# Graph kernel on one Trainium2 core: x also given with features on partitions, its norm summed on TensorE, the counts stored from ScalarE's queue

## The chip, the cores and the metric

One core of one Trainium2 chip runs the whole program. The metric is the device time of one execution in microseconds (us); the kernel before takes 937.81 us as the median of 3 runs (936.04 to 939.39). The engines are called as the profile calls them: PE (TensorE, with PEld for its weight loads), DVE (VectorE), ACT (ScalarE), POOL (GpSimd) and SP (SyncE, which here only issues DMAs). "SPq" and "ACTq" are the parts of SP and ACT that issue.

## What is computed

Two graph layers over 6250 nodes with 128 features and 200000 edges that are sorted by `dst`, each followed by a layer norm:

```python
h = x @ W + b_W;  xi, xj = split(h, 2)
xji = xj[src] + (edge_attr @ W_e + b_We)
xji = xji / (in_degree[dst] + 1e-6)
x1  = layernorm(x + xi + segment_sum(xji, dst))          # layer 0

h   = x1 @ W1                                            # layer 1, with self loops
out = segment_sum(h[src] * dinv[src] * dinv[dst], dst) + b1
y   = leaky_relu(batchnorm(out) * gamma + beta)
return layernorm(x1 + y)
```

What the change touches belongs to layer 0: the own part `x + xi`, which is one product of `x` with (W + identity), and the split of `x` into two float16 parts (high and low), which needs a power of two as a common scale.

## The kernel before

The 6250 nodes lie in 25 blocks (NB) of 256 receivers; `x` is kept in SBUF as 49 tiles (HS) of 128 nodes. For each block the kernel builds a matrix of counts, how many edges go from each sender to each receiver of the block: for 16 steps ("slots", `s` = 0 to 15) DVE makes pairs of one-hot tiles (`one_hots`, L616 and L619, one pair of instructions for two slots, in a ring of 6 slots), PE multiplies them (`count`, L858, 8 matmuls for a slot), and ACT writes the result as bf16 into `counts` (`pair_out`, L1065). There are two buffers `counts`, for even and odd blocks. While block b is counted, PE multiplies the counts of block b-1 with the split x (`product`, L876, and L884 for the parts of layer 1 that can be done early), and sums the edges' features (`edges`, L895). The counts of each block also go to HBM (`counts_kept`), since layer 1 reads them again; `pair_out` of block b, slot 0, must wait until the store of block b-2 has landed, as it writes the same buffer. After block 24 comes a stretch in which PE gathers layer 1 from the kept counts (`gather_z`, L951), and then the output.

The order on each engine is the order in which the functions are called in its loop over b and s; nothing is planned by a scheduler. Every engine runs its own list and waits at semaphores. What the change touches:

- **The start, before block 0.** SP loads rows of `dst` (`load_rows`, L301), weights and the first third of x. `find_below` and `pick_rows` (DVE L557, L562), `find_rows` (PE L911), `count_row` and `start_of` (DVE L569 to L576) find where the edges of a block start; POOL then gathers a window of `dst` and `src` (L465), and `make_keys` (DVE L582 to L602), `turn_keys` (PE L921) and `tables` (ACT L1089) make the keys from which `one_hots` works.
- **The own part.** x lies with nodes on partitions, so PE turns each tile (`turn_x`, L972), ACT copies it from PSUM (`x_turned`, L1137), PE multiplies it with the weights (`own_product`, L981), and ACT copies the result into `zown` (`own_out`, L1142); 13 groups of up to 4 tiles (OWN), four of them before block 0 and the rest one per slot of block 0. One PSUM bank, `j_ps`, takes all the products.
- **The scale.** DVE takes the largest absolute value of each row (`largest`, L646, three pieces of x), PE turns the column of largest values (L1007), DVE makes four numbers of it (`scales`, L655 to L663), PE spreads them over the partitions (L1010) and DVE copies them (`spread_scales`, L668). Then ACT writes the high part of each third of x (`split_high`, L1130) and DVE the low part (`split_low`, L681).
- **SP's list for block b:** rows for block b+4, then `start_values`, `load_destinations` (L333), `keep_inverse` (L370), `keep_counts(b-1)` (L349), the first half of the edges' features (`load_edges`, L342), and the second half. The second half of block 0 waits for the last `split_low`, because its buffer is the one that holds x.

## Time and profile before

| | us |
|---|---|
| median of 3 runs | 937.81 |
| the profiled execution, its own time | 936.68 |
| the span that the profile covers | 934.6 |
| PE busy in it | 883.9 (95%) |
| DVE busy | 676.6 (72%) |
| ACT busy | 450.3 (48%) |
| POOL busy | 349.4 (37%) |

The profile is one execution, taken by the hardware profiler. It gives the busy time of each engine, the clock that TensorE was granted, the groups of instructions by line with the idle time before them and what ended it, and for any stretch the instructions in order of time. Times count from the start of the span. 2.1 us of the execution's time lie outside the span. A matmul's end is modelled, so neighbouring matmuls overlap in the list; the distance of their starts is what they cost.

### The profile page before, as it was taken

What the parts mean: (1) busy time and instruction counts of PE and PEld (TensorE: products, weight loads), DVE (VectorE), ACT (ScalarE), POOL (GpSimd) and SP (SyncE); (2) the same over time, 40 slices, a digit from 0 to 9 for tenths busy, and PEclk for the clock granted to TensorE, in tenths of its full rate; (3) what the DMA queues carried; (4) which work ended last, traced back from release to release, by engine and by line L of the source; (5) the groups of instructions that cost most, each with busy time, mean ns of one, the idle gap of its engine ahead of it and who ended that gap; (6) DMA issues with size and microseconds to landing.
All of it is one profiled execution on the core that took longest, in us unless ns stands there. A gap on an engine that the chain in (4) does not pass through costs nothing.

```text
span 934.6 us, 30500 instructions
## 1 busy us (share of the span) xinstructions
PE 883.9 (95%) x12210; PEld 791.2 (85%) x12210; DVE 676.6 (72%) x1249; ACT 450.3 (48%) x983; POOL 349.4 (37%) x401
## 2 busy tenths in 40 slices
PE   4867999999999999999999999999999999999995
PEld 4756888888988898989899999999988888888874
DVE  6999899999999998899888899888842111112255
ACT  3764666656666665556565556565542000000026
POOL 2236444455554444455334455434332011112200
PEclk8988999999999999999999999999999999999998
DMA  6428999998879788777878758678667897779654
GB/s 180 110 83 296 361 345 320 317 342 290 313 247 319 284 311 283 229 229 241 253 264 277 223 185 301 214 274 282 209 216 299 343 358 279 272 260 326 249 155 136
DMA packets 96762, 244.77 MB, mean 262 GB/s; under 512 B 39560, under 2 KB 64838, under 8 KB 90726
## 3 DMA queue, kind: packets, MB, share of 16 engines
q1 hardware_dynamic: 95014, 239.46, 73.7%
q0 software_dynamic: 1600, 3.28, 1.4%
q8 instruction: 100, 1.64, 0.8%
q14 instruction: 48, 0.39, 0.2%
HBM read 183.85 MB, written 58.85 MB: 260 GB/s over the span
## 4 chain that ended last, share of the span: by engine, by line
PE 85%; DVE 5%; issue 3%; ACT 3%; DMA 1%; SPq 1%; ACTq 0%; DVEq 0%
PE x_ps L876 26%; PE pair_ps L951 19%; PE pair_ps L858 13%; PE e_ps L895 10%; PE x_ps L884 9%; PE j_ps L933 2%; PE j_ps L981 2%; DVE lo_oh L616 1%; DVE key_oh L619 1%; PE pair_ps L960 1%; PE j_ps L934 1%; ACT counts L1065 1%; PE u_vps L1409 1%; DMA counts_kept<-counts 1%; DMA streams<-in_x 1%
## 5 line engine op out<-in xcount | busy, mean ns | idle before, releaser
L1065 ACT CAST counts<-pair_ps 128x784 bf16<-128x784 f32 x391 | 315.3, 817 | 251.5 <-PE pair_ps L858 244.1
L876 PE MATMUL x_ps<-counts,xsplit 128*128 128x256 bf16 (+1 forms) x2450 | 307.5, 271 | 0.0
L616 DVE TENSOR_TENSOR lo_oh<-counter,lo_t 128x2048 bf16<-128x2048 bf16 x196 | 252.3, 1287 | 53.9 <-PE pair_ps L858 52.5
L876 PEld LDWEIGHTS x_ps<-counts,xsplit 128*128 128x128 f16 x2450 | 222.1, 98 | 29.3 <-issue 7.1
L858 PE MATMUL pair_ps<-key_oh,lo_oh 128*128 128x100 bf16 x3128 | 207.8, 209 | 22.5 <-ACT counts L1065 15.4
L858 PEld LDWEIGHTS pair_ps<-key_oh,lo_oh 128*128 128x128 bf16 x3128 | 182.8, 98 | 36.9 <-issue 15.0
L619 DVE TENSOR_TENSOR key_oh<-counter,key_t 128x1600 bf16<-128x1600 bf16 x196 | 196.4, 1002 | 0.0
L895 PE MATMUL e_ps<-streams 128*32 128x128 f32 x3528 | 106.9, 274 | 0.1
L884 PE MATMUL x_ps<-counts,zown 128*128 128x256 bf16 (+1 forms) x840 | 105.9, 269 | 0.1
L951 PE MATMUL pair_ps<-streams,zown 128*128 128x256 bf16 x878 | 99.0, 273 | 0.0
L895 PEld LDWEIGHTS e_ps<-streams 128*32 128x32 f32 x3528 | 93.3, 110 | 4.8 <-issue 1.0
L476 POOL TENSOR_SCALAR quot<-deg 128x2 f32<-128x2 f32 x25 | 5.7, 226 | 243.2 <-DVE junk L595 231.5
L951 PEld LDWEIGHTS pair_ps<-streams,zown 128*128 128x128 f16 x878 | 85.8, 98 | 11.4 <-issue 0.2
L884 PEld LDWEIGHTS x_ps<-counts,zown 128*128 128x128 f16 x840 | 76.1, 97 | 10.3 <-issue 2.9
L492 POOL TENSOR_SCALAR bias<-linear,share 128x128 f32<-128x128 f32 x50 | 76.0, 1532 | 14.7 <-DVE vo L705 13.7
L951 PE MATMUL pair_ps<-counts,zown 128*128 128x256 bf16 (+1 forms) x732 | 79.9, 268 | 0.0
L951 PEld LDWEIGHTS pair_ps<-counts,zown 128*128 128x128 f16 x732 | 69.3, 98 | 9.2
L1313 ACT ACTIVATE u_co<-u_co 128x1 f32<-128x1 f32 x1 | 0.2, 203 | 156.0 <-DVEq L1351 156.0
L825 DVE TENSOR_TENSOR s_mem<-pair_ps,key_oh 128x256 f32<-128x256 f32 (+1 forms) x23 | 9.6, 418 | 83.8 <-PE pair_ps L951 81.3
L639 DVE TENSOR_TENSOR streams<-iota,ekeys 128x1152 f32<-128x1152 f32 x49 | 67.5, 1377 | 2.7 <-PE e_ps L895 0.3
L833 DVE TENSOR_TENSOR xsplit<-pair_ps,key_oh 128x256 f32<-128x256 f32 (+1 forms) x25 | 10.5, 419 | 58.7 <-PE pair_ps L960 57.0
L507 POOL TENSOR_TENSOR streams<-streams,key_oh 128x512 bf16<-128x512 bf16 x13 | 15.0, 1151 | 84.9 <-DMA streams<-counts_kept 84.9
(181 smaller groups left out, 890.6 us busy)
## 6 DMA issues: line engine op xcount, KB each, us to landing
streams<-in_edge_attr SPq DMA_DIRECT2D x196, 576.0 KB, 9.1
counts_kept<-counts SPq DMA_DIRECT2D x10, 1600.0 KB, 9.1
streams<-counts_kept SPq DMA_DIRECT2D x6, 1600.0 KB, 6.5
counts<-counts_kept SPq DMA_DIRECT2D x4, 1600.0 KB, 7.1
counts_kept<-counts SPq DMA_DIRECT2D x2, 3136.0 KB, 12.7
streams<-counts_kept SPq DMA_DIRECT2D x2, 3136.0 KB, 14.8
edst<-in_dst SPq DMA_DIRECT2D x196, 4.5 KB
streams<-in_x SPq DMA_DIRECT2D x3, 1024.0 KB, 5.7
```

Of the source, the lines that this page charges most:

```text
L492: last = g.tensor_scalar(bias[:, t, :], bje, share[:, 2 * b + t:2 * b + t + 1], None, ALU.mult)
L616: dv.tensor_tensor(lo_oh[:, ring, :, :, :].rearrange("p r w k t -> p (r w) k t"), counter[:, :, :].unsqueeze(1).to_broadcast([P, g, P, 2]) ...
L619: dv.tensor_tensor(key_oh[:, ring, :, :, :].rearrange("p r w k t -> p (r w) k t"), counter[:, 0:KW, :].unsqueeze(1).to_broadcast([P, g, KW ...
L639: dv.tensor_tensor(e_oh[g][:, :, :], iota[:, 0:EC].unsqueeze(1).to_broadcast([P, EG * EJ, EC]), ekeys[:, k].unsqueeze(2).to_broadcast([P, ...
L858: last = nc.tensor.matmul(pair_ps[at % 2][:, half_of, col:col + KW], lo_oh[:, at % RING, w // 2, :, w % 2], key_oh[:, at % RING, w // 2, : ...
L876: last = nc.tensor.matmul(x_ps[:, 0, 0:n], xsplit[:, q // 2, q % 2, :], by_hi[:, q // 2, :], start=(q == 0), stop=(q == 2 * HS - 1))
L884: last = nc.tensor.matmul(x_ps[:, 1, 0:n], zsplit[:, z // 2, z % 2, :], by_hi[:, z // 2, :], start=(z == 0), stop=(z == early(k) - 1))
L895: last = nc.tensor.matmul(e_ps[EC * c:EC * (c + 1), g, :], e_oh[g][:, c * EJ + j, :], ebuf[g][:, c, j, :], start=(j == 0), stop=(j == EJ - 1))
L933: nc.tensor.matmul(out, sx[:, t:m:2], wj, start=True, stop=False)
L951: last = nc.tensor.matmul(z_ps[i % 2][:, 0:n], zsplit[:, q // 2, q % 2, :], by_hi[:, q // 2, :], start=(q == early(b)), stop=(q == 2 * HS ...
L981: last = nc.tensor.matmul(j_ps[:, k, :], xT[m % 2][:, k, :], wi, start=True, stop=True)
L1065: a.copy(out.rearrange("p h (g n) -> p h g n", g=2), pair_ps[at % 2][:, :, 0:4 * KW].rearrange("p g (n h) -> p h g n", h=HI)[:, 0:HS]).the ...
```

## The change

1. The host hands x over in two more layouts, both as 49 tiles: `x_rows` (nodes on partitions, as before) and `x_columns` (features on partitions). SP loads both, the columns first, straight into `zown`; the memset of x's last tile on POOL goes.
2. The own part takes its tiles from `x_columns`: `turn_x` and `x_turned` go, and the products alternate between two PSUM banks (`j_ps` and `e_ps`), each followed by `own_out` into the place that the columns held. One group stands ahead of block 0, the other twelve in slots 0 to 11.
3. The scale comes from the norm of x: PE multiplies the upper bf16 half of each column tile with itself and adds up all 49 products in one bank (`sum_squares`), DVE sums the diagonal (`add_squares`), PE adds it over the partitions (one matmul with ones), and DVE makes the scales on all partitions (`scales`). `largest` in block 0 goes; `row_largest` reads the high parts in blocks 16, 18 and 20 instead.
4. The splits stand earlier: ACT's in slots 9, 12, 15 (were 11, 13, 15), DVE's in 14, 17, 20 (were 16, 18, 20).
5. `find_below` and `pick_rows` of blocks 2 and 3, with ACT's and PE's parts, move ahead of the first own product.
6. `keep_counts(b-1)` moves from SP's queue to ACT's, at slot 0 of block b, ahead of `pair_out`.
7. Rows are loaded one turn sooner, at another place of SP's list; `count_row` and `start_of` move from slots 9 and 10 to 11 and 12.

```diff
-LARGEST_AT = (None, 2, 4)
-TOP_AT, SCALES_AT, SPREAD_AT = 5, 8, 12
-HIGH_AT, LOW_AT = (11, 13, 15), (16, 18, 20)
+NORM_AT, TOTAL_AT, SCALES_AT = 7, 6, 10
+HIGH_AT, LOW_AT = (9, 12, 15), (14, 17, 20)
+ROWS_CHECKED_AT = (16, 18, 20)
-OWN_FIRST = 4
+SQUARED_FIRST, OWN_FIRST = 4, 1
+SQUARED_IN = {1: (4, 5, 6, 7), 3: (8, 9, 10, 11, 12)}
...
+def load_pieces(sp, out, table, loaded, pieces):
     for k in pieces:
+        at = piece_tiles(k)
+        sp.dma_start(out[:, at.start * F:at.stop * F], table[:, at.start * F:at.stop * F]).then_inc(loaded[k], 16)
...
+        own_ps = [j_ps, e_ps]
+        squares_ps, norm_ps = x_ps[:, 0, 0:P], x_ps[:, 1, 0:1]
+        upper_halves = zown[:, :].bitcast(BF16).rearrange("p (h n q) -> p h n q", n=P, q=2)[:, :, :, 1]
...
             for b in range(2):
                 load_rows(sp, b)
-            sp.dma_start(wi, W0[:, 0:F]).then_inc(S["wi_in"], 16)
-            load_inputs(sp, {"x": xf}, x, S, range(1))
+            load_pieces(sp, columns, x_columns, S["columns_in"], range(1))
             for b in range(2, ROW_RING):
                 load_rows(sp, b)
+            sp.dma_start(wi, W0[:, 0:F]).then_inc(S["wi_in"], 16)
             load_weights(sp, {"wj": wj, "we": we, "bi": bi, "bj": bje, "be": be_t[:, :]}, W0, b0, We, be, S)
             sp.wait_ge(win_in[0], 32)
-            load_inputs(sp, {"x": xf}, x, S, range(1, len(X_PIECES)))
+            load_pieces(sp, columns, x_columns, S["columns_in"], range(1, len(X_PIECES)))
+            load_pieces(sp, xf, x_rows, S["x_in"], range(len(X_PIECES)))
...
-                if 1 <= b <= NB - 2:
-                    keep_counts(b - 1)
...
+            def add_squares():
+                dve.wait_ge(S["squares_summed"], 1)
+                step(dv.tensor_tensor(x1_mem[:, 0, :], squares_ps, ident[:, :], ALU.mult))
+                dv.tensor_reduce(out=norm[:, :], in_=x1_mem[:, 0, :], axis=AX.X, op=ALU.add).then_inc(S["norm_ready"], 1)
...
+            def row_largest(k):
                 at = piece_tiles(k)
+                step(dv.tensor_reduce(out=rowmax[:, at], in_=xsplit[:, at, 0, :], axis=AX.X,
+                                      op=ALU.max, apply_absolute_value=True))
...
+            def sum_squares(m):
+                columns_here(m)
+                h, n = OWN[m]
+                for k in range(h, h + n):
+                    last = nc.tensor.matmul(squares_ps, upper_halves[:, k, :], upper_halves[:, k, :], start=(k == 0), stop=(k == HS - 1))
+                last.then_inc(S["columns_squared"], 1)
...
             def own_product(m):
                 h, n = OWN[m]
+                columns_here(m)
                 pe.wait_ge(S["weights_ready"], 1)
-                pe.wait_ge(S["xT_out"], m + 1)
-                reach(pe, S["own_added"], m)
+                reach(pe, S["own_added"], m - 1)
                 for k in range(n):
-                    last = nc.tensor.matmul(j_ps[:, k, :], xT[m % 2][:, k, :], wi,
-                                            start=True, stop=True)
+                    last = nc.tensor.matmul(own_ps[m % 2][:, k, :], own[:, h + k, :], wi, start=True, stop=True)
...
-            for b in range(2):
+            for b in range(ROW_RING):
                 find_rows(b)
-            for m in range(OWN_FIRST):
-                turn_x(m)
-                if m >= 1:
-                    own_product(m - 1)
+            for m in range(SQUARED_FIRST):
+                sum_squares(m)
+                if m < OWN_FIRST:
+                    own_product(m)
             turn_keys(0)
-            for b in range(2, 4):
-                find_rows(b)
-            own_product(OWN_FIRST - 1)
...
+            def keep_counts(k):
+                act.wait_ge(S["pair_out"], first_slot(k) + slots(k))
+                at, n = early(k) // 2 * cols(k), HS * cols(k)
+                act.dma_start(scratch["counts"][k * P:(k + 1) * P, at:n], counts[k % 2][:, at:n])\
+                   .then_inc(counts_kept[k % 2], 16)
...
+                    if s == 0 and 1 <= b <= NB - 2:
+                        keep_counts(b - 1)
                     if b < NB and s < slots(b):
                         pair_out(b, s)
```

How the instructions of one engine stand in its list, before and with the change, at three places. First PE, from its start to the second slots of block 0. The old list (L911 finds rows, L972 turns x, L981 is the own product, L921 and L922 turn the keys, L858 counts a slot):

```order
L911 MATMUL pair_ps<-rows,pick 128x129 x2
L972 MATMUL x_ps<-ident,streams 128x128 x4
L972 MATMUL e_ps<-ident,streams 128x128 x4
L981 MATMUL j_ps<-linear,x_mem 128x128 x4
L972 MATMUL x_ps<-ident,streams 128x128 x4
L981 MATMUL j_ps<-linear,s_mem 128x128 x4
L972 MATMUL e_ps<-ident,streams 128x128 x4
L981 MATMUL j_ps<-linear,x_mem 128x128 x4
L921 MATMUL keys_ps<-ident,key 128x128
L922 MATMUL keys_ps<-ident,lo 128x128
L911 MATMUL pair_ps<-rows,pick 128x129 x2
L981 MATMUL j_ps<-linear,s_mem 128x128 x4
```

The new list (L886 finds rows, L948 squares, L960 is the own product, L896 and L897 turn the keys, L831 counts):

```order
L886 MATMUL pair_ps<-rows,pick 128x129 x4
L948 MATMUL x_ps<-zown 128x128 x4
L960 MATMUL j_ps<-linear,zown 128x128 x4
L948 MATMUL x_ps<-zown 128x128 x12
L896 MATMUL keys_ps<-ident,key 128x128
L897 MATMUL keys_ps<-ident,lo 128x128
L831 MATMUL pair_ps<-key_oh,lo_oh 128x100 x8
L960 MATMUL e_ps<-linear,zown 128x128 x4
L831 MATMUL pair_ps<-key_oh,lo_oh 128x100 x8
L948 MATMUL x_ps<-zown 128x128 x16
L960 MATMUL j_ps<-linear,zown 128x128 x4
L831 MATMUL pair_ps<-key_oh,lo_oh 128x100 x8
```

Ahead of the keys stand four tiles of the own part instead of twelve, no tile is turned, and all four row products come first; 16 and 17 of the squares stand in slots 1 and 3 of block 0.

Second DVE, block 0 from its second pair of one-hots to the first low part. The old list (L616 and L619 a pair of one-hots, L646 the rows' largest values, L655 to L663 the scales, L668 their copy, L681 the low part; the ten instructions of the keys and the repeated pairs are left out):

```order
L646 TENSOR_REDUCE rowmax<-streams 128x17
L650 TENSOR_REDUCE pmax<-rowmax 128x1
L616 TENSOR_TENSOR lo_oh<-counter,lo_t 128x2048
L619 TENSOR_TENSOR key_oh<-counter,key_t 128x1600
L616 TENSOR_TENSOR lo_oh<-counter,lo_t 128x2048
L619 TENSOR_TENSOR key_oh<-counter,key_t 128x1600
L655 TENSOR_REDUCE top<-keys_ps 1x1
L656 TENSOR_SCALAR expo<-top 1x1
```

The new list from its fifth pair (L597 and L600 a pair, L625 and L626 the diagonal, L630 to L638 the scales):

```order
L625 TENSOR_TENSOR x_mem<-x_ps,ident 128x128
L626 TENSOR_REDUCE norm<-x_mem 128x1
L597 TENSOR_TENSOR lo_oh<-counter,lo_t 128x2048
L600 TENSOR_TENSOR key_oh<-counter,key_t 128x1600
L597 TENSOR_TENSOR lo_oh<-counter,lo_t 128x2048
L600 TENSOR_TENSOR key_oh<-counter,key_t 128x1600
L630 COPY top<-x_ps 128x1
L631 TENSOR_SCALAR sound<-top 128x1
```

The reductions over 2048 and 2176 elements are gone from between the pairs of block 0; two instructions over 128 elements stand in their place.

Third ACT, from the ninth slot of block 0 to the first slots of block 1. The old list (L1065 writes counts, L1130 the high part, L1151 and L1152 rows for a later block, L1083 a root):

```order
L1151 ACTIVATE heads<-rows_i,shift 128x2
L1152 ACTIVATE rows<-rows_i,shift 128x128
L1065 CAST counts<-pair_ps 128x49x16
L1130 ACTIVATE xsplit<-streams,xscale 128x16x128
L1065 CAST counts<-pair_ps 128x49x16 x2
L1130 ACTIVATE xsplit<-streams,xscale 128x16x128
L1065 CAST counts<-pair_ps 128x49x16 x2
L1130 ACTIVATE xsplit<-streams,xscale 128x17x128
L1065 CAST counts<-pair_ps 128x49x16 x3
L1083 ACTIVATE quot<-quot 128x2
```

The new list (L1033 writes counts, L1105 the high part, L1112 copies an own product, L1121 and L1122 rows, L1046 the store):

```order
L1105 ACTIVATE xsplit<-streams,xscale 128x16x128
L1033 CAST counts<-pair_ps 128x49x16
L1112 COPY zown<-e_ps 128x512
L1121 ACTIVATE heads<-rows_i,shift 128x2
L1122 ACTIVATE rows<-rows_i,shift 128x128
L1033 CAST counts<-pair_ps 128x49x16
L1112 COPY zown<-j_ps 128x128
L1033 CAST counts<-pair_ps 128x49x16
L1105 ACTIVATE xsplit<-streams,xscale 128x16x128
L1033 CAST counts<-pair_ps 128x49x16 x3
L1105 ACTIVATE xsplit<-streams,xscale 128x17x128
L1046 DMA counts_kept<-counts 128x12544
```

All three high parts now stand in block 0, the first of them ahead of six slots' counts, and the store of block 0's counts follows the last of them on ACT itself.

## Rows read from the trace of the kernel before

**Rows 1.** Busy time by stretch: PE, PEld, DVE, ACT, POOL (instructions), PE clock, DMA share, GB/s.
```profile
24.00:25.00 1.00, 0.94 (x7) 0.81 (x4) 1.00 (x1) 0.92 (x2) 0.00 (x0) 0.50 0.09 5
88.00:89.00 1.00, 0.25 (x4) 0.28 (x5) 1.00 (x2) 1.00 (x2) 0.92 (x2) 0.50 1.04 428
150.00:175.00 25.00, 24.23 (x398) 21.75 (x397) 24.75 (x45) 16.78 (x35) 12.97 (x15) 1.00 0.90 322
400.00:425.00 25.00, 25.00 (x397) 22.83 (x396) 21.59 (x33) 14.37 (x30) 11.31 (x12) 1.00 0.74 233
```

**Rows 2.** DVE in order of time: start, us, line, what, [idle before <-releaser].
```profile
11.14 0.23 DVE L582 TENSOR_SCALAR bit_i<-gsrc 128x128 int32<-128x128 int32 x1 [0.75 <-DMA gsrc<-in_src,start_i]
16.87 0.29 DVE L557 TENSOR_SCALAR below<-even,heads 128x128 f32<-128x128 f32 x1 [3.88 <-ACT rows L1152]
...
19.54 1.22 DVE L616 TENSOR_TENSOR lo_oh<-counter,lo_t 128x2048 bf16<-128x2048 bf16 x1
...
23.61 2.28 DVE L646 TENSOR_REDUCE rowmax<-streams 128x16 f32<-128x2048 f32 x1
...
29.66 2.41 DVE L646 TENSOR_REDUCE rowmax<-streams 128x17 f32<-128x2176 f32 x1
...
43.63 0.16 DVE L668 COPY xscale<-keys_ps 128x4 f32<-128x4 f32 x1 [1.78 <-PE keys_ps L1010]
...
48.49 2.35 DVE L681 SCALAR_TENSOR_TENSOR xsplit<-streams,xscale,xsplit 128x2048 f16<-128x2048 f32 x1 [0.50 <-ACT xsplit L1130]
...
63.46 1.36 DVE L616 TENSOR_TENSOR lo_oh<-counter,lo_t 128x2048 bf16<-128x2048 bf16 x1
...
87.32 1.12 DVE L619 TENSOR_TENSOR key_oh<-counter,key_t 128x1600 bf16<-128x1600 bf16 x1
...
95.35 0.35 DVE L569 TENSOR_SCALAR_CACHE_REDUCE row_junk<-keys_ps,th 128x128 bf16<-128x128 f32 x1 [1.44 <-ACT lo_t L1090]
...
99.67 1.27 DVE L616 TENSOR_TENSOR lo_oh<-counter,lo_t 128x2048 bf16<-128x2048 bf16 x1 [0.40 <-PE pair_ps L858]
```

**Rows 3.** PE in order of time, in block 0 and at the start of block 2.
```profile
18.48 1.95 PE L981 MATMUL j_ps<-linear,s_mem 128*128 128x128 f32 x8
...
29.48 1.13 PE L981 MATMUL j_ps<-linear,x_mem 128*128 128x128 f32 x8 [0.41 <-ACT x_mem L1137]
30.44 0.60 PE L972 MATMUL e_ps<-ident,streams 128*128 128x128 f32 x4
...
88.75 0.83 PE L858 MATMUL pair_ps<-key_oh,lo_oh 128*128 128x100 bf16 x8 [4.55 <-ACT counts L1065]
```

**Rows 4.** ACT in order of time: the first high part, and the start of block 2.
```profile
46.45 2.01 ACT L1130 ACTIVATE xsplit<-streams,xscale 128x2048 f16<-128x2048 f32 x1
...
87.80 1.53 ACT L1065 CAST counts<-pair_ps 128x784 bf16<-128x784 f32 x2 [5.61 <-issue]
```

**Rows 5.** SP's queue in order of time: block 0's edges, and the first store of counts.
```profile
30.68 34.96 SPq L342 DMA_DIRECT2D streams<-in_edge_attr  x8
...
75.47 0.43 SPq L349 DMA_DIRECT2D counts_kept<-counts  x1
```

**Rows 6.** DMA issues from 75 to 100 us, KB each, median us to landing.
```profile
counts_kept<-counts SPq DMA_DIRECT2D x2, 3136.0 KB, 12.7
```

**Rows 7.** SP's issues of the store, then of rows: ns min/median/max.
```profile
L349 SPq DMA_DIRECT2D counts_kept<-counts x23: 430/431/1789, 75.5 to 659.3; - x23
L301 SPq DMA_DIRECT2D rows_i<-in_dst x23: 398/442/2570, 0.7 to 509.4; - x23
```

**Rows 8.** Waits of all engines, 100 to 150 us, then 500 to 600: total, times, longest.
```profile
DVE lo_oh L616 <- PE pair_ps L858: 2.7, 3, 2.1
DVE lo_oh L616 <- PE pair_ps L858: 13.2, 8, 2.7
```

**Rows 9.** ACT, then PE, at a later block's start.
```profile
455.41 1.56 ACT L1065 CAST counts<-pair_ps 128x784 bf16<-128x784 f32 x2
457.47 0.53 PE L858 MATMUL pair_ps<-key_oh,lo_oh 128*128 128x100 bf16 x8
```

197 lines of the change are left out of this document (77 added, 120 removed).

## The prediction

> **What bounds the kernel now.** I read the busy time by stretch first [rows 1]; the reader should see that the bound changes: from 150 to 175 us DVE is busy 24.75 of 25 us, from 400 to 425 us only 21.59, while PE is then busy for all 25.00. So up to about 200 us DVE sets the pace, behind it PE, and a microsecond won on DVE early moves everything after it, since PE starts each block when its one-hots are there. I then followed DVE in order of time [rows 2]. It starts block 0 at 19.54 us and from there to 93.8 us stands still only twice for more than a tenth: 1.78 us for PE's answer to the scales and 0.50 us for ACT's first high part. The point I measure against is 63.46 us, where the last low part is done and the pair of slot 6 in block 1 starts; from there DVE's list is the same before and after, but for small moves.
>
> Later PE shows its one long stop, 4.55 us ahead of 88.75 [rows 3]. ACT, for which it waits, itself stood 5.61 us and began at 87.80 [rows 4]. The view calls that "issue", but ACT's list has a wait there for the store of block 0's counts. SP issued that store only at 75.47, since its list was held in block 0's edges from 30.68 for 34.96 us [rows 5]; with 12.7 us to landing [rows 6] it lands at about 88.2, or a little before. So the store is what PE waited for.
>
> **Start of block 0.** Before: keys at 11.14, done 1.85 us later at 12.99; then DVE stood 3.88 us until 16.87, because ACT's copies of the turned x stood ahead of the rows of blocks 2 and 3; 2.67 us of row work; first pair at 19.54 [rows 2]. Now that row work starts as soon as the rows land. The piece of columns has the size of the piece of x and should land at the same 8 us; rows and weights are queued behind it, so I put the row work at 9.0 to 10.4, the weights' four instructions (1.1 us) to 11.6, the keys to 13.4, the two counts of rows (1.3 us) beside PE's and ACT's work on the keys, and the first pair at 14.9. **-4.6 us.** Bounds: -5.2 if the keys start at 11.14 as before, -3.5 if one own product at the low clock (1.95 us for four tiles [rows 3]) lies ahead of the keys in full.
>
> **Work taken from DVE in block 0.** The second and third `largest` (2.28 and 2.41 us [rows 2], with the reduction behind the third 5.0 in all): **-5.0**. The first, at 8.1, lay beside the wait for the gather and is worth nothing. The wait for the scales goes with its copy (2.07, of which 1.78 is the wait) and so do eight small instructions (1.08); in come two instructions over 128 elements and six small ones, 1.55 together by their like: **-1.6**. The 0.50 us for the first high part goes with its neighbours, **-0.6**. Sum so far -11.8.
>
> **What is late next.** PE and ACT. PE's slot in block 0 before was an own product and a turn, 0.96 us from start to start (29.48 to 30.44), and a slot's count of 0.37, drawn out to 2.34 by waits on ACT [rows 3]. Without the turns and with two banks it is 0.96 + 0.37 = 1.33 us for 12 slots. The 33 squares of slots 1 and 3 have no row of their own. The lower bound is a 128-column matmul of 16 bits, 0.05 us, the upper one a turned tile of 32 bits, 0.11 (0.44 for four, behind [rows 3]'s 0.60). I take 0.055, since they are 16-bit: 1.8 us. The clock also counts: it was 0.50, the lower of its levels (1.2 GHz), at 24 to 25 us [rows 1], after PE had idled around 17 us, and at that level an own product took 1.95 against 1.13 [rows 3]. I let PE run 4 us from 17 us at that level. PE's slot 9 is then counted at 33.3, two slots behind DVE. ACT writes it, copies a product (about 0.5, as PE's wait of 0.41 for such a copy tells) and only then makes the first high part (2.01 [rows 4]), done at 37.3. DVE is ready for it at 35.4: 1.9 us of new wait. Before the second high part it waits some 0.7 more, and for a free place of the ring and the diagonal 0.9. **+3.5**; bounds 0 and 6. At my point the sum is -8.3: 55.2 instead of 63.46.
>
> **The store.** Now on ACT behind block 0's last count, at about 47 us, where DMA is nearly idle, and landed long before block 2. The 4.55 us of PE go, and the clock, which had fallen to 0.50 at 88 us [rows 1], stays up. But that isn't the gain. PE would next want the one-hots of slot 4, and DVE, busy throughout, has them only at 88.4 (87.32 and 1.12 [rows 2]). What is gained is what DVE stood still in consequence: 1.44 and 0.40 [rows 2] and the longest wait on PE in 100 to 150 us, 2.1 [rows 8]: **-3.9**. Bounds: 0 and -6.9 (the stop and 2.3 us of slow clock in full).
>
> **Costed at nothing.** Each store now takes ACT one issue, 0.43 us as on SP [rows 7], and a wait for its own last count. Behind it stand the next counts, for which PE waits two slots later: at a later block's start ACT has the first of two done at 456.2 (half of 1.56 after 455.41), and PE takes it up at 457.47 [rows 9], so 1.2 us cover it; without cover 23 x 0.43 = 10 us. The three `row_largest` (2.3 us each) fall in blocks 16, 18 and 20, where DVE waits for PE 13.2 us in 100 [rows 8]; without that cover, 6.9. The 3.1 MB of second layout run from 11 to 28 us, ahead of any edge's feature that is wanted. Rows a turn sooner, and the row counts two slots later, are waited for by nobody.
>
> **Sum.** -8.3 - 3.9 = -12.2 against the profiled 936.7 (span 934.6 and 2.1 outside), so 924.5; the median of the runs lies 1.1 above the profiled run, so 925.6.
>
> **A rule against it.** The store's gain rests on it being issued some 28 us sooner, by SP's rows [rows 5]. The Trainium skill ("DMA: Bandwidth & Descriptors", "Issuing engines are not separate DMA queues") says that DMAs from several engines run on the same 16 DMA engines and that issuing from more than one only saves issue time. By that alone the move would be worth nothing, and the sum be -8.3. The trace doesn't contradict the rule, it shows a case outside of it: what held the store was a wait in SP's list.
>
> **Rivals.**
> - *Clean overlap:* PE and ACT keep up, the 3.5 us of new waits don't come. For it: ACT loses its turned copies. Against it: 16 counts at 0.77, 12 copies at 0.5 and the three high parts (2.0 to 2.1, [rows 4]) give ACT 24.5 us of work, to DVE's 22. 922.1.
> - *The store brings nothing:* DMA was at 1.04 of its share at 88 us [rows 1], and if the edges of blocks 1 and 2 hold PE there in the store's place, only -8.3 is left: 929.5.
> - *The gather of block 1 comes late:* 5.2 MB of x now run while it does. DVE wants it at 18.9; if it landed only with the last of x, near 26, 7.5 us of the gain would go: 933.1. Against it: POOL issues it ahead of those pieces, for which SP waits until 11.1.
> - *PE's clock stays low through block 0:* twice 19.3 us from 17 gives 55.5 for its last count instead of about 51, and with the store's gain nothing is left: 938. Against it: PE has fewer gaps than before, and before the clock was back by 27 us.
> - *Slower:* the issue on ACT holds it longer than the cover. One of 23 on SP took 1.79 us, and one of its issues of rows 2.57 [rows 7]. It decides from 1.2 + 12.2 / 23 = 1.7 us for each store. At 2.6 it costs 1.4 x 23 = 32, so 957. Against it: the median is 0.431 [rows 7], and ACT has a queue to itself.
>
> **Chances.** Forecast 0.50; clean overlap 0.17; store brings nothing 0.15; late gather 0.08; slow clock 0.05; slower 0.05. The range goes from 919 (3 us under clean overlap, for the bounds of the start and the store) to 933, and leaves out the last two and half of the late gather. No change is within 0.3% (2.8 us), about what a measurement of this kernel can tell: slow clock, 0.05; faster 0.90; slower 0.05.
>
> **What would show it.** In the new profile: first pair of one-hots near 14.9 us; all low parts done near 55; DVE's waits in block 0 on ACT's high parts, some 3 us, and none on a matmul for the scales; no stop of PE near the start of block 2, and a clock of 1.00 there; the store issued from ACT near 47 us with 0.43 us an issue; PE without idle time from 400 us on, as before. It is wrong if DVE waits on the gather in block 0, if ACT's issues exceed 1 us, or if PE shows waits on ACT at each block's start behind 400 us.

## The result, and the profile after

The changed kernel takes **943.59 us** as the median of 20 runs (936.97 to 950.21); the kernel before, run beside it on the same chip, 937.51 (20 runs, 935.10 to 941.11). The ratio is 1.0064, 95% interval 1.0047 to 1.0081: **slower by 0.64%**, where 925.6 and 90% for faster were forecast. The profiled execution took 947.89 us, with a span of 946.1, of which PE is busy 884.7 (883.9 before), DVE 675.2 and ACT 444.7. So none of these three has more to do; PE waits more. (POOL shows 392.3 against 349.4, but PE waits for it nowhere, and DVE 1.4 us at the start, as before.) Two steps of the forecast can be looked up at once.

**The start came out as forecast.** DVE in order of time, the columns being those of [rows 2]:

```profile
15.06 1.23 DVE L597 TENSOR_TENSOR lo_oh<-counter,lo_t 128x2048 bf16<-128x2048 bf16 x1 [0.67 <-ACT lo_t L1064]
...
25.43 0.29 DVE L625 TENSOR_TENSOR x_mem<-x_ps,ident 128x128 f32<-128x128 f32 x1 [0.32 <-PEq L952]
...
28.57 1.23 DVE L597 TENSOR_TENSOR lo_oh<-counter,lo_t 128x2048 bf16<-128x2048 bf16 x1 [0.49 <-PE pair_ps L831]
...
37.56 2.35 DVE L655 SCALAR_TENSOR_TENSOR xsplit<-streams,xscale,xsplit 128x2048 f16<-128x2048 f32 x1 [1.35 <-ACT xsplit L1105]
...
42.72 2.35 DVE L655 SCALAR_TENSOR_TENSOR xsplit<-streams,xscale,xsplit 128x2048 f16<-128x2048 f32 x1 [0.77 <-ACT xsplit L1105]
...
53.03 2.47 DVE L655 SCALAR_TENSOR_TENSOR xsplit<-streams,xscale,xsplit 128x2176 f16<-128x2176 f32 x1
55.43 1.35 DVE L597 TENSOR_TENSOR lo_oh<-counter,lo_t 128x2048 bf16<-128x2048 bf16 x1
```

The first pair stands at 15.06 (forecast 14.9, before 19.54), the pair behind the last low part at 55.43 (forecast 55.2, before 63.46). The new waits shown, 0.32 + 0.49 + 1.35 + 0.77 = 2.9 us, are those that the forecast put at 3.5; a fifth, 0.54 us on ACT for a root at 31.86, it had not named.

**The stop of block 2 is gone.** Its slot 0 is counted at 73.58 with a wait of 0.63 us, where PE stood 4.55 [rows 3]; its slot 5 at 81.52, 13.1 us ahead of before. Then comes what the forecast did not have. PE in order of time:

```profile
73.58 0.52 PE L831 MATMUL pair_ps<-key_oh,lo_oh 128*128 128x100 bf16 x8 [0.63 <-ACT counts L1033]
...
81.52 0.53 PE L831 MATMUL pair_ps<-key_oh,lo_oh 128*128 128x100 bf16 x8
88.40 4.07 PE L870 MATMUL e_ps<-streams 128*32 128x128 f32 x72 [6.35 <-issue]
92.40 1.34 PE L849 MATMUL x_ps<-counts,xsplit 128*128 128x256 bf16 x7
```

PE stands 6.35 us, and no engine or DMA is named as what ended it: "issue" means a wait for nothing that the profile shows. The 72 matmuls behind the stop take 4.00 us from start to start instead of the 2.1 of elsewhere; the granted clock from 88 to 92 us is 0.50, the lower of the two levels (1.2 GHz), after the engine had stood. There are ten stops with "issue" as their end, 17.7 us in all, between 82 and 560 us. The waits of the whole execution (engine, tile and line, releaser: total, times, longest), first of the changed kernel, then of the one before:

```profile
PE e_ps L870 <- issue: 14.7, 8, 6.4
PE x_ps L849 <- issue: 1.9, 1, 1.9
PE pair_ps L831 <- issue: 1.0, 1, 1.0
```

```profile
PE pair_ps L858 <- issue: 1.2, 1, 1.2
```

They are of two kinds.

**Two stand at the head of a group of edge matmuls** ("x72"), 6.35 us at 88.40 and 2.13 at 177.65, 8.5 in all. There the program has a wait: `edges` waits until the edges' features have landed. The profile doesn't name it; in this execution it gives no landing time for these loads. The row of the DMA issues, which before ended in a median of 9.1 us:

```profile
streams<-in_edge_attr SPq DMA_DIRECT2D x196, 576.0 KB
```

SP issued the first group's edges of block 1 from 69.10 on, ACT the store of block 1's counts (3.1 MB) at 73.47, with the edges still on their way. SP's and ACT's queue in order of time:

```profile
69.10 2.16 SPq L331 DMA_DIRECT2D streams<-in_edge_attr  x4
```

```profile
73.47 0.33 ACTq L1046 DMA_DIRECT2D counts_kept<-counts  x1
```

The kept trace also has each increment of the semaphore for which `edges` waits, 64 for the four loads of a group. The last one for this group came at 88.31 us, 0.09 us before PE went on at 88.40; for the second stop it came at 177.56, again 0.09 us ahead of 177.65. So both are waits for edges. p_slot4 below shows such a stop with its name.

**The eight others, 9.2 us, lie inside groups**, with 1, 2, 4, 4, 20, 31, 53 and 70 matmuls of the group to go, where the program has no wait. The busy time by stretch of the changed kernel, cut at stops (columns of [rows 1]):

```profile
118.00:142.30 24.30, 23.43 (x372) 20.94 (x372) 23.12 (x44) 16.40 (x34) 15.76 (x14) 1.00 0.93 314
...
186.00:211.60 25.60, 22.95 (x373) 20.52 (x373) 22.45 (x43) 15.41 (x31) 15.80 (x14) 1.00 0.92 307
211.60:238.10 26.50, 24.25 (x373) 21.58 (x372) 24.17 (x44) 15.15 (x30) 15.79 (x14) 0.94 0.88 299
238.10:281.00 42.90, 40.85 (x619) 36.90 (x620) 37.73 (x73) 27.19 (x55) 22.98 (x24) 1.00 0.86 281
281.00:307.20 26.20, 25.11 (x372) 22.54 (x372) 22.55 (x44) 16.43 (x34) 11.31 (x14) 1.00 0.86 263
```

Between two of them lie 744 to 746 matmuls and weight loads, or 1239, five thirds of that. (The stop at 88.40 is off this grid, 909 from the next one, and so is that at 177.65, with 1013 before it and 233 behind; both are of the first kind.) With the waits at semaphores, which stand in PE's list as instructions of their own, the steps are 768 and 1280, or 3 and 5 times 256. Data and buffers don't come in steps of 256 instructions; the instructions themselves do, if they are fetched in pieces of fixed size. The DMA queues of the changed kernel (packets, MB, share of 16 engines' span):

```profile
q1 hardware_dynamic: 89338, 193.20, 64.3%
q10 hardware_dynamic: 3312, 49.48, 12.3%
q0 software_dynamic: 1600, 3.28, 1.3%
q8 instruction: 100, 1.64, 0.7%
q14 instruction: 49, 0.39, 0.2%
```

q8 carries "instruction": 100 packets of 16384 bytes, 1.64 MB in all, which is 64 bytes for each of 256 instructions. The trace has the time of each packet. The stop that ends at 118.12 us ends 1.5 us after one of them (115.77 to 116.65), and so do the seven others, 1.2 to 1.5 us after; at 88.40 and 177.65 the last packet of q8 is 6.6 to 6.7 us old. The same holds for the experiments below: of the 100 stops that their table counts as within groups, in all kernels together, 99 end 1.2 to 1.7 us after a packet of q8 and stand a whole number of 256 instructions apart in PE's list (the other is one of 0.24 us in j_half_store). So PE's instructions come by DMA, and these stops are **instruction fetches that come late**. q10, 3312 packets of 15 KB on average, is new: the stores that ACT issues, before a part of q1.

Where the time is lost: block 4's first group of edges stands at 165.81 us (168.14 before), block 6's at 224.63 (219.43), block 10's at 333.95 (323.74), and behind that the two kernels run in step, 10 us apart (block 15's at 472.51 and 462.46). The gain of some 13 us at 82 us, and 10 more, go between there and 330 us, where the DMA engines have least to spare: their share from 150 to 200 us is 0.95, from 400 to 425 it is 0.82.

### The profile page after: what moved, and what is told of

Its sections match the earlier page's. It is cut to its first block, busy times and chain, and to the rows that moved or that the text cites. A ratio compares the mean times of both kernels' runs of the same rounds, so it can differ in the third digit from the quotient of the medians.

```text
span 946.1 us, 30473 instructions
## 1 busy us (share of the span) xinstructions
PE 884.7 (94%) x12209; PEld 791.2 (84%) x12209; DVE 675.2 (71%) x1245; ACT 444.7 (47%) x970; POOL 392.3 (41%) x400
## 3 DMA queue, kind: packets, MB, share of 16 engines
q10 hardware_dynamic: 3312, 49.48, 12.3%
q8 instruction: 100, 1.64, 0.7%
## 4 chain that ended last, share of the span: by engine, by line
PE 85%; DVE 5%; issue 4%; ACT 3%; DMA 2%; SPq 0%; ACTq 0%; DVEq 0%
PE x_ps L849 26%; PE pair_ps L926 17%; PE pair_ps L831 14%; PE e_ps L870 11%; PE x_ps L857 9%; PE j_ps L908 2%; DVE key_oh L600 1%; ACT counts L1033 1%; PE j_ps L909 1%; DMA key_oh<-sums_z 1%; PE pair_ps L935 1%; DVE lo_oh L597 1%; PE u_vps L1376 1%; PE j_ps L960 1%; DMA rows_i<-in_dst 1%
## 5 line engine op out<-in xcount | busy, mean ns | idle before, releaser
L1033 ACT CAST counts<-pair_ps 128x784 bf16<-128x784 f32 x391 | 315.6, 817 | 271.5 <-PE pair_ps L831 250.7
L597 DVE TENSOR_TENSOR lo_oh<-counter,lo_t 128x2048 bf16<-128x2048 bf16 x196 | 247.0, 1260 | 69.6 <-PE pair_ps L831 68.4
L831 PE MATMUL pair_ps<-key_oh,lo_oh 128*128 128x100 bf16 x3128 | 207.3, 208 | 20.5 <-ACT counts L1033 11.1
L831 PEld LDWEIGHTS pair_ps<-key_oh,lo_oh 128*128 128x128 bf16 x3128 | 182.2, 98 | 34.6 <-issue 16.5
L600 DVE TENSOR_TENSOR key_oh<-counter,key_t 128x1600 bf16<-128x1600 bf16 x196 | 198.8, 1014 | 0.0
L870 PE MATMUL e_ps<-streams 128*32 128x128 f32 x3528 | 112.2, 279 | 14.8 <-issue 14.7
L870 PEld LDWEIGHTS e_ps<-streams 128*32 128x32 f32 x3528 | 97.0, 112 | 19.1 <-issue 15.4
L473 POOL TENSOR_SCALAR bias<-linear,share 128x128 f32<-128x128 f32 x50 | 72.5, 1456 | 14.6 <-DVE vo L679 13.7
L619 DVE TENSOR_TENSOR streams<-iota,ekeys 128x1152 f32<-128x1152 f32 x49 | 67.1, 1369 | 3.2 <-PE e_ps L870 0.8
L475 POOL TENSOR_TENSOR bias<-bias,linear 128x256 f32<-128x256 f32 x25 | 55.6, 2225 | 2.1
L806 DVE TENSOR_TENSOR xsplit<-pair_ps,key_oh 128x256 f32<-128x256 f32 (+1 forms) x25 | 10.5, 419 | 58.6 <-PE pair_ps L935 57.1
```

The source lines that it names most:

```text
L473: last = g.tensor_scalar(bias[:, t, :], bje, share[:, 2 * b + t:2 * b + t + 1], None, ALU.mult)
L475: g.tensor_tensor(bias[:, :, :], bias[:, :, :], bi.unsqueeze(1).to_broadcast([P, 2, F]), ALU.add).then_inc(S["bias_ready"], 1)
L597: dv.tensor_tensor(lo_oh[:, ring, :, :, :].rearrange("p r w k t -> p (r w) k t"), counter[:, :, :].unsqueeze(1).to_broadcast([P, g, P, 2]) ...
L600: dv.tensor_tensor(key_oh[:, ring, :, :, :].rearrange("p r w k t -> p (r w) k t"), counter[:, 0:KW, :].unsqueeze(1).to_broadcast([P, g, KW ...
L619: dv.tensor_tensor(e_oh[g][:, :, :], iota[:, 0:EC].unsqueeze(1).to_broadcast([P, EG * EJ, EC]), ekeys[:, k].unsqueeze(2).to_broadcast([P, ...
L831: last = nc.tensor.matmul(pair_ps[at % 2][:, half_of, col:col + KW], lo_oh[:, at % RING, w // 2, :, w % 2], key_oh[:, at % RING, w // 2, : ...
```

## The experiments

The theories after this first look. **Q, the second queue:** stores from ACT's queue run beside the edges' loads of SP's instead of in one line with them, and edges and instruction fetches come late. **T, the moment:** wherever it is issued, the store now goes ahead of the destinations and edges of its block instead of behind them. Each kernel ran five rounds, beside the kernel before, whose median lay between 935.76 and 938.10 from batch to batch; so ratios to it are compared, of which 0.001 is 0.94 us. The last column has PE's waits on "issue" between 40 and 760 us in the one profiled execution, which can lie several us off the median (c's is the longest of 12): those at the head of a group of edges, and all others, which nearly always stand within a group. Waits that the profile names as a DMA are not in it: 1.5 us in e, 1.3 in o, 0.5 in i, 5.3 in p.

| kernel | stores of counts | ratio to before (95%) | median us | stops, head + within |
|---|---|---|---|---|
| before | SP, behind destinations | 1 | 937.51 | 0 + 1.2 |
| changed | ACT, block's end | 1.0064 (1.0047 to 1.0081) | 943.59 | 8.5 + 9.2 |
| a_sp_store | SP, old place | 0.9928 (0.9906 to 0.9949) | 931.15 | 0 + 3.7 |
| b_act_store (before's x) | ACT, block's end | 1.0176 (1.0139 to 1.0214) | 953.92 | 4.9 + 10.5 |
| c_small_packets | ACT, 4 KB packets | 1.0012 (0.9996 to 1.0028) | 939.26 | 5.1 + 10.2 |
| d_late_store | ACT, slot 8 | 1.0070 (1.0045 to 1.0095) | 944.54 | 3.7 + 3.1 |
| e_sp_head | SP, head of its turn | 1.0001 (0.9987 to 1.0015) | 935.10 | 0 + 6.6 |
| **f_first_on_act** | block 0's on ACT, others SP, old place | **0.9888** (0.9872 to 0.9903) | **925.47** | 0 + 2.9 |
| g_before_small (before's x) | ACT, 4 KB packets | 1.0099 (1.0077 to 1.0120) | 943.84 | 0 + 5.5 |
| i_before_head (before's x) | SP, head | 1.0173 (1.0159 to 1.0187) | 952.30 | 0 + 9.3 |
| j_half_store | half of each ACT, half SP | 0.9938 (0.9913 to 0.9963) | 932.72 | 3.2 + 6.3 |
| k_late_blocks | as f, from block 10 on ACT | 0.9906 (0.9876 to 0.9937) | 929.68 | 0 + 5.1 |
| l_sp_tail | as f, SP behind both groups of edges | 1.2965 (1.2924 to 1.3006) | 1216.82 | 0 + 0 |
| m_sp_between | as f, SP between the groups | 1.0097 (1.0065 to 1.0130) | 945.93 | 0.5 + 1.0 |
| n_first_small | as f, 4 KB packets | 0.9875 (0.9857 to 0.9892) | 925.63 | 0 + 2.0 |
| o_head_small | as e, 4 KB packets | 0.9997 (0.9975 to 1.0019) | 936.99 | 0.6 + 7.5 |
| p_slot4 | ACT, slot 4 | 0.9986 (0.9960 to 1.0012) | 934.36 | 0 + 5.1 |

### The two halves of the change

a_sp_store: the changed kernel with the store back in SP's list; b_act_store: the kernel before with only the store moved.

```diff
# a_sp_store, against the changed kernel: on ACT
-                    if s == 0 and 1 <= b <= NB - 2:
-                        keep_counts(b - 1)
# on SP
+                if 1 <= b <= NB - 2:
+                    keep_counts(b - 1)
                 if b < NB:
                     load_edges(b, 0, starts)
# b_act_store, against the kernel before: the same lines the other way round
```

> The changed kernel with one part undone: the stores of the counts are issued by SP again, at their old place. Theory Q (the store on a queue of its own is served between the packets of the edges' features and of PE's instructions, one of its packets of some 22 KB against one of theirs of 4.6 KB or less, and so makes PE wait): the waits of PE called issue fall from 17.6 us to under 3, the start keeps its gain of 8 us, the stall at block 2 is partly back, 926 to 932. Theory X (the new start or SP's new order costs it): it stays at 940 or more. Theory R (the DMA engines are simply short of throughput once the blocks start sooner): 936 to 942, PE's waits for edges stay.

> The kernel before with only the stores of the counts moved to ACT's queue at slot 0. Theory Q: the stall ahead of 88 us goes, but waits of PE called issue come up in blocks 1 to 9, 15 us or more in sum, so slower than before, 941 to 950. Theory X: 932 to 936, since the store alone is harmless. Theory R: between, 934 to 939.

The part on x alone is a gain of 0.72% (6.7 us), the store alone a loss of 1.8% (16.5 us; 953.9 is above the 941 to 950 of theory Q), with stops of both kinds: 4.85 us at the head of a group at 97.28, then within groups 1.61, 2.63 and 2.30. In a_sp_store the first edges stand at 54.53 us against 62.80, the forecast's 8.3 to the tenth; at 400 us 5.6 of them are left. The two halves don't simply add: in the changed kernel the same move of the store costs 12.8 us (1.0064 against 0.9928), not 16.5.

### Packets, and a later slot

c_small_packets and g_before_small leave a gap of 128 bytes behind every eight tiles of kept counts in HBM, so that a store goes out in packets of 4 KB instead of 12.8 (the late blocks) to 25.1 (the first two). d_late_store issues from ACT at slot 8 of the block instead of 0.

```diff
# c, g
-                act.dma_start(scratch["counts"][k * P:(k + 1) * P, at:n], counts[k % 2][:, at:n])
+                for kept, part, q in kept_parts(scratch["counts"][k * P:(k + 1) * P, :], at // BN):
+                    ours = counts[k % 2][:, part]
+                    act.dma_start(kept, ours if q is None else ours.rearrange("p (g q) -> p g q", q=q))
# d
-                    if s == 0 and 1 <= b <= NB - 2:
+                    if s == 8 and 1 <= b <= NB - 2:
```

> The changed kernel, the stores still on ACT's queue at slot 0, but the kept counts laid out in HBM with 128 bytes of padding behind every 8 tiles, so that a packet holds 4 KB and not 25 KB (two issues for each store and each load). Theory Q, if the size of the packets is what matters: most of PE's waits go, 924 to 934. If only the number of queues matters, or theory R: as the changed kernel, 940 to 946.

> The changed kernel with the store on ACT's queue at slot 8 of the next block instead of slot 0, about when SP issued it before. Theory Q: the packets still come between, so the waits only move, 938 to 946. A theory T (it is the time of the store, in front of the edges that are due next, that matters): waits fall, 926 to 934.

> The kernel before with the stores on ACT's queue at slot 0, kept with padding so that a packet holds 4 KB. The large packets gave 953.9. Theory Q with the size of packets as a part of it: 940 to 948, a third to two thirds of the 17 us come back, as 4 to 5 of the changed kernel's 12 did. If the size doesn't matter: 950 to 957.

Small packets give back 4.9 us (c) and 7.2 us (g): in g the stops fall from 15.3 to 5.5 us, in c, whose profile is 3.0 us shorter than the changed kernel's, from 17.7 to 15.3. That is part of the loss at most; c lies between its two expectations. d's time is in theory Q's range, but not for Q's reason: its stops fall to 6.7, and still it is no faster. ACT in order of time:

```profile
135.92 1.53 ACT L1033 CAST counts<-pair_ps 128x784 bf16<-128x784 f32 x2 [3.66 <-DMA counts_kept<-counts]
```

The store of block 2, issued at 120.50, lands at 135.9, 15.4 us later, and ACT has to wait for it before it writes that buffer again; seven such waits make 11.7 us. Slot 8 is too late for a store that takes this long beside the edges.

### The moment, on one queue

All stores from SP's queue, at the head of its turn, so ahead of the destinations and edges, nearly as early as from ACT (block 0's at 56.8 us instead of 45.2, block 1's at 77.4 instead of 73.5): e_sp_head with the changed kernel's x, i_before_head with that of before. And f_first_on_act: only the store of block 0 from ACT, where no edges run, the other 22 in the old place.

```diff
# e, i, on SP
             for b in range(NB + 2):
+                if 1 <= b <= NB - 2:
+                    keep_counts(b - 1)
                 if b < NB:
                     starts = start_values(b)
# f, on ACT; SP keeps those of blocks 1 to 22 ahead of load_edges(b, 0)
+                    if s == 0 and b == 1:
+                        keep_first_counts()
```

> The changed kernel with all stores back on SP's queue, but each at the head of SP's turn, ahead of the values, destinations and edges. Theory Q (interleaving of two queues costs it, the early store itself is good): the stall at block 2 goes and nothing comes between the packets, the start's 8 us and most of the 3.9 are kept, 924 to 928. Theory T (a store ahead of the edges costs it, on whatever queue): 932 or more, PE waits for edges.

> The kernel before with only its stores moved to the head of SP's turn: the stall ahead of 88 us alone. Theory Q, with the price of 3.9 us from the prediction: 932 to 935.5. If the stall was worth nothing, or SP's list then becomes late: 936 or more.

> The changed kernel with only block 0's store on ACT's queue (issued near 45 us, with nothing else in flight) and the 22 others on SP's at their old place. Theory Q: one store that meets no other traffic costs nothing and takes the stall away, 924 to 929. If a second queue costs by being used at all, or if starting block 2 sooner only brings PE to edges that aren't there: 931 or more.

f is 1.12% under the kernel before, the most of all but n_first_small below, which equals it, and it **shows the two gains of the forecast together**: 3.7 us more than a_sp_store (by the intervals, 1.3 to 6.2), for the stop at block 2 that was put at 3.9. At the same place in its program PE doesn't stop. PE in order of time, the group that stood at 88.40 above:

```profile
81.67 0.53 PE L839 MATMUL pair_ps<-key_oh,lo_oh 128*128 128x100 bf16 x8
82.12 2.17 PE L878 MATMUL e_ps<-streams 128*32 128x128 f32 x72
```

Fetches still come late at the same places: f stops at 108.96, 133.02, 195.75 and 220.53 us, with the same 1, 20, 2 and 4 matmuls to go as in the changed kernel at 118.12, 142.44, 211.73 and 238.21, for 0.21, 0.17, 0.84 and 1.72 us instead of 1.53, 0.66, 1.94 and 1.79.

Against f, moving the 22 others costs 16.5 us (0.0176). e says how this divides: 10.6 us (0.0113) come without a second queue, by the moment, 5.9 (0.0063) with the queue. The division is rough, since e's stores also start some us later than the changed kernel's. But **Q alone is refuted** (it had 924 to 928 for e), **and T alone too**, as long as those few us are not what makes the 5.9. The heads of groups tell what the second queue does: on one queue (e) the store of block 1 stands behind the edges that were issued before it, and PE waits for edges once, 1.5 us; from ACT it runs beside them, and the wait is 8.5. i is as slow as b, but its trace has a cause of its own. ACT in order of time:

```profile
84.82 0.30 ACT L1151 ACTIVATE heads<-rows_i,shift 128x2 f32<-128x2 int32 x1 [10.93 <-DMA rows_i<-in_dst]
```

Here the rows, 64.5 KB that SP issues at 66.84, stand in the queue behind the edges (64.17 to 66.25) and 3.1 MB of store, and ACT, which turns them into numbers in the same block, waits 10.93 us for them; there are six such waits between 40 and 760 us, 17.2 us in all, about i's whole loss of 16.2. In e, whose rows are loaded a turn sooner, they are missing. The part of the change that I had costed at nothing is what an early store on this queue needs.

### How much of it, and when

j_half_store: of each later store half the bytes from ACT at the block's end, half from SP in the old place. k_late_blocks: as f, but from block 10 on (about 330 us) all of it from ACT.

```diff
# j, on ACT; SP stores half:n in the old place, and waits count 32 for a block
+                half = (at + n) // 2
+                for a0, a1 in [(at, half), (half, n)][:1 if k else 2]:
+                    act.dma_start(scratch["counts"][k * P:(k + 1) * P, a0:a1], counts[k % 2][:, a0:a1])
# k, on ACT
+                    if s == 0 and (b == 1 or 11 <= b <= NB - 2):
+                        keep_counts(b - 1)
```

> As the kernel with block 0's store alone on ScalarE's queue (925.5), but of every later store half of the bytes leave from ScalarE's queue at the block's end and the other half from SyncE's at the old place behind the destinations. Moving all of the bytes cost 18.1 us (943.6). Theory Q+T (it is the volume that runs ahead of and beside the edges and beside the instruction fetches): between, about half, 931 to 938. If the mere presence of a second queue decides: nearly the whole, 940 to 944. If the harm needs the long store (8 us of all engines) to outlast something: 925 to 928.

> As the kernel with block 0's store alone on ScalarE's queue (925.5), and the stores of blocks 10 to 22 (issued from about 330 us on) there too: 14 of 23 stores moved. The trace of the changed kernel lost its time between 82 and 300 us, where the DMA engines are busy 90 to 100% of the time. Theory load (a moved store only hurts where the engines are full): 925 to 928. Theory price per store (0.8 us for each of 22): 935 to 937.

Half of the bytes costs 4.7 us over f, 28% of the whole, with stops of 9.5: the mere presence of a second queue isn't it, the volume counts. The 13 late stores cost 1.7 us (the intervals of k and f overlap: anything from nothing to 5), the nine early ones the rest of the 16.5. That is 0.1 us for a late one and some 1.6 for an early one, so no fixed price per store. The early ones are larger (2.1 to 3.1 MB, against 1.6 to 2.0), but not by as much; that the fuller DMA engines make the rest fits their shares above, and is not shown by itself.

### Later places on SP's queue

l_sp_tail stores behind both groups of edges, m_sp_between behind the first.

```diff
# m; l has the same two lines behind load_edges(b, 1)
                     load_edges(b, 0, starts)
+                if 2 <= b <= NB - 2:
+                    keep_counts(b - 1)
```

> As the kernel with block 0's store alone on ScalarE's queue (925.5), the others on SyncE's queue at the end of the turn, behind both groups of edges. Theory order (what is behind the store in the queue is delayed by it; next is then the next block's destinations, some 10 us later): 924 to 927. If the store comes too late for the counts' buffer two blocks on, ScalarE waits for its landing at block starts: 930 to 945.

> As before, the others between the two groups of edges on SyncE's queue: the first group no longer waits behind the store. Theory order: 924 to 927, the best place if the first edges are what is late; if the old place was only good because of its time, no change within 0.3% (923 to 928).

I had expected these to be at least as good as f. m has 945.9, outside of both its ranges, and l is slower by 30%, by the cause that its second theory named, but far above its 930 to 945. Waits of l_sp_tail, and ACT in order of time in it:

```profile
PE pair_ps L839 <- ACT counts L1041: 252.2, 41, 15.8
...
ACT counts L1041 <- DMA counts_kept<-counts: 248.2, 21, 15.9
```

```profile
156.70 1.53 ACT L1041 CAST counts<-pair_ps 128x784 bf16<-128x784 f32 x2 [15.72 <-DMA counts_kept<-counts]
```

21 of 22 stores land too late for their buffer, by 11.8 us on average, and it seems to feed itself: the second group of edges waits for a buffer that PE frees only when it goes on. m has eight such waits, 15.3 us, and hardly any stop of the other kind (1.5 us). The old place, behind the destinations and ahead of the edges, is thus between two losses: earlier, fetches and loads are held up; later, the counts' buffer.

### Packets once more

With the length of the packets still open, at the good place and at the early one on one queue (edit as in c, with the placing of f and e):

> As the kernel with block 0's store alone on ScalarE's queue (0.9888 of before), but the counts are kept in HBM with a gap of 128 bytes behind every eight tiles, so that the packets of the stores are 4 KB instead of about 15 to 22 KB. On SyncE's queue, in the old place. If the length of a packet is what another queue's fetch waits behind, whatever the place: 0.984 to 0.988, a little better, as fetch stops of 2.9 us are left to win. If it matters only where stores run beside the edges: 0.987 to 0.991. If more packets cost in themselves: above 0.992.

> As the kernel with all stores at the head of SyncE's turn (1.0001 of before), with packets of 4 KB. One queue, the same early moment as in the changed kernel. If long packets at that moment are what holds up the instruction fetches: down to 0.989 to 0.994. If it is the bytes that go ahead of the destinations and edges, whatever their packets: 0.998 to 1.003.

Neither differs clearly from its pair with long packets (0.9875 and 0.9888; 0.9997 and 1.0001, intervals overlapping). On one queue the length of the packets makes no difference; only with the second queue did short ones give something back.

### A slot between

What was left: what the stops at the heads of groups are, and whether ACT's queue has a good slot between 0 and 8. The edit is d's, with slot 4.

> As the changed kernel, stores from ScalarE at slot 4 of the block (slot 0: 1.0064, slot 8: 1.0070). Two kinds of stops in the traces: those at the head of a group of 72 edge matmuls, where the program has a wait for the edges' landing (6.35 and 2.13 us in the changed kernel), and those in the middle of groups, on the grid of some 248 instructions (9.2 us). Theory of two costs: at slot 4 block 0's store has landed before block 1's edges are issued, so the 6.35 us and the landing waits of slot 8 (11.7 us) go, and the stops in the middle of groups stay as long as the second queue is there: 0.994 to 0.999. Theory that the second queue alone sets the price, wherever the store stands: 1.003 to 1.009. Theory of the moment alone: near the kernel with SP at the old place, 0.989 to 0.993.

It came out at 0.9986, in the range of the two costs and of neither other theory. The 6.35 us at block 1's first group and the 11.7 us of landing waits are gone, 5.1 us within groups remain, and one stop has moved, this time with its name. PE in order of time:

```profile
69.97 4.07 PE L870 MATMUL e_ps<-streams 128*32 128x128 f32 x72 [5.34 <-DMA streams<-in_edge_attr]
```

It is block 0's second group; SP issues its edges from 54.68 on, when x's last low part is done, beside the store of block 0's counts, which ACT issued at 52.76. So here too the stop at the head of a group is a wait for edges that run beside a store. The best of the three slots tried on ACT's queue still costs more than the old place on SP's: 9.2 us over f.

## Why the prediction was wrong

- **Start of block 0 (-4.6), work taken from DVE (-5.0, -1.6, -0.6), new waits (+3.5):** right. The sum was 55.2 us at the point of measure, the trace has 55.43, and a_sp_store, with 55.20, has the 8.3 us. That it is so close is in part luck: the new waits came 0.6 us cheaper than put, and one of 0.54 us that was not forecast made up for it. Of the 8.3, a_sp_store's runs keep 6.7; PE has stops of its own on the way (3.7 us against 1.2).
- **The store (-3.9):** right for block 0's store, 3.7 us by f against a, though the interval is as wide as 1.3 to 6.2. The rule of the Trainium skill that I weighed against it ("DMA: Bandwidth & Descriptors", "Issuing engines are not separate DMA queues") would have made it nothing; here what held the store was SP's list, and f shows the gain. But the rule names only the issue time as what a move changes. The runs show that moving 22 more cost 16.5 us.
- **Costed at nothing:** here the prediction failed. "Each store now takes ACT one issue" looked at the sequencer only. The issue is indeed cheap (326 to 362 ns, covered, no wait of PE on ACT behind it). What I left out is what the store does on the DMA engines: 22 stores of up to 3.1 MB go ahead of the loads of their block, at a DMA share that my own rows gave as 0.90 [rows 1], beside a second queue, and edges (8.5 us of stops) and PE's instructions (9.2 against f's 2.9) come late. Measured: **+16.5 us**, some 10.6 for the moment and 5.9 for the second queue, where I had put 0. I had costed the move as that of one store, since one store stood on the path, and the 22 others by their issue time alone. "ACT has a queue to itself" even stood among the arguments against a loss; it is where the 5.9 come from.
- **The slower rival** had the right sign and the wrong mechanism: it needed 1.7 us of issue time for each store, which is 0.33. That an early store did cost some 1.6 us is chance.
- **The others:** the gather of block 1 was not late (its keys start at 19.14 without a wait), and ACT's and PE's waits in block 0 were there, so no clean overlap. "The store brings nothing" (929.5) falls by f; but what it feared, edges that hold PE in the store's place, is what happened at 88.40 us once all stores were moved. PE's clock did not stay low in block 0, it was 1.00 at 24 to 25 us, but fell behind the stops: 0.91 over 70 to 110 us, 0.97 over 150 to 200.
- **What would show it:** the signs of the start and of the first slots of block 2 were there (clock 1.00 over 70 to 82 us, the store issued at 45.2), and none of the three signs of being wrong came, since I had asked of the store only whether its issue was short. What failed is the clock and the idle time of PE between 82 and 330 us, for which I had named nothing.

f_first_on_act, the change as the forecast had imagined it, runs at 0.9888 of before; 925.6 was 0.9870 of the 937.81 before.

**What stays open.** How the early moment costs 10.6 us on one queue is known in the main. e's profile is 6.0 us longer than f's, and 5.2 of them are stops: 3.7 within groups (6.6 against 2.9) and 1.5 in a wait for edges. The rest of the 10.6 lies mostly between profiles and medians: e's profiled execution is 2.1 us under its median, f's 1.6 above. What makes the fetches late under load is less clear: o rules out only the packets' length, and no run varied the fetches themselves. How the 16.5 us divide between moment and queue rests on e, whose stores don't start quite as early. Of "rows a turn sooner" only its use beside an early store is seen, by comparing e with i, which also differ in x.

## What to carry to other kernels

When one transfer of a series is on the critical path, move that one: block 0's store gave 3.7 us, the 22 others cost 16.5. A DMA's price in a full stretch is not its issue but what stands behind it and beside it, so look up the DMA share where each instance of it will run, and look for what it has to be ahead of (here the buffer's next use) and behind (the loads that are wanted first); the window between may be one place wide. And if PE stops with "issue" as the releaser, look at where in its group the stop stands: at the head a semaphore may be behind it that the profile couldn't name, in the middle count the instructions between such stops, and look for a packet of an instruction queue just ahead of each.

## What the runs showed of the hardware

- **PE's instructions arrive by DMA while it runs, and can come late.** 100 packets of 16384 bytes on a queue of their own, one for 256 instructions of PE's list; 99 stops of PE within groups, in 16 of the 17 kernels (before among them), all at such a step and all 1.2 to 1.7 us after such a packet; 1.2 us in all in the kernel before and 10.5 in b. Of the pieces 8 to 34 (about 100 to 330 us) PE reached the first instruction 3.7 us after its packet in the median before, 3.4 in f, 3.0 in e and 2.4 in the changed kernel. The Trainium skill ("DMA: Bandwidth & Descriptors", "Queues, rings and completion order") says that a DMA engine goes round the queues that have work, a packet at a time, so that a fetch would wait for a packet of each other queue. The traces agree in part: at the early moment the stops within groups are 9.2 us with two data queues and 6.6 with one, with before's x 10.5 and 9.3. They do not bear out that the length of the profile's packets sets it: c has 10.2 with 4 KB. Whether these are the packets of which that page speaks, no run here shows.
- **A stop costs more than itself.** Behind the stop of 6.35 us the granted clock was 0.50 (1.2 GHz) over 88 to 92 us, and 72 matmuls took 4.00 us from start to start instead of 2.1; behind the one of 2.13 us they took 3.16.
- **Behind on one queue, beside on two.** Edges issued from 69.10 on, 4.4 us ahead of a store from another queue, had landed only at 88.31. With the store behind them on the same queue (e: edges from 70.89, store at 77.43) their last increment came at 82.99, and with the store issued only at 86.14 (f: edges from 69.29) at 81.02. A store of 3 MB took 15.4 us to land beside the edges (d), 12.7 before [rows 6].
- **"issue" as a releaser can hide a DMA:** the same wait of PE at the head of a group is "issue" in the changed kernel, where the profile has no landing times for the edges, and "DMA streams<-in_edge_attr" in p_slot4. The increments of the semaphore, which the trace keeps, told it: seven such stops in six kernels end 0.09 us after the last one.
- **The spread was larger in most kernels with all stores on ACT's queue:** the 20 runs of the changed kernel span 13.2 us, six of b 13.1, twelve of p 12.4; the 20 of the kernel before 6.0, f's four 2.9. It isn't the stops alone: i, with 9.3 us of them on one queue, spans 2.5 in five runs, o, with 7.5, 10.1 in twelve.
